# Low half stacked under the high half in the first inverse step: two products per group in place of three

## The chip, the cores and the metric
One core of a Trainium2 chip runs the whole program in one launch. The metric is device time in microseconds (us), the median of several executions. PE is TensorE (matmul), PEld its weight load, DVE VectorE, ACT ScalarE, POOL GpSimd, SP SyncE.

## The reference, cut to what matters
The program computes a Fourier attention layer on 128 images of 128 x 128, then an attention and an expert layer over tokens. The change touches only the inverse transforms of the first layer, which come three times (the projection, the first mixer layer and the second one):

```
def spectral_conv(x, w, out_shape):
    ...
    out_ft = out_ft.at[:, :, :mh, :mw].set(top)
    out_ft = out_ft.at[:, :, -mh:, :mw].set(bot)
    return jnp.fft.irfftn(out_ft, s=out_shape, axes=(-2, -1), norm='forward')
```

Of each image 34 x 34 real coefficients are kept (17 cosines and 17 sines in each direction). The inverse is two small matrix products: columns first (34 coefficients to 128 pixels), then rows.

## The kernel before, in words
`build` runs twelve stages, each a block with a barrier at its end. Three of them are `stage_inverse` with `kind` 'proj', 'mix1' and 'mix2'. Every value that needs more than half precision is held as two float16 parts, a high one and the low rest, and a product of two such values is three products: high by high, high by low, low by high.

A `stage_inverse` has this order:

- Head. In 'proj' alone DVE first sums the squares of the coefficients (L1345), PE spreads the sum over partitions, DVE and ACT make a scale of it. Then PE turns the coefficients, 34 transposes in nine banks (L1201). ACT copies each bank as float16 into `coefH` (L1251) and DVE writes the rest into `coefL` (L1355). Both lie on partitions 0 to 33 of the tile `spare`, one behind the other.
- First step, `first(q)`, for quads q = 0 to 10. A quad is four groups of three images (the last has fewer). Each group has three products with 34 contraction rows and 102 output rows: `coefH` by `colsH`, `coefH` by `colsL`, `coefL` by `colsH`, of 128 columns each, accumulated in one bank (L1166 to L1168). So a full quad has 12 matmuls, each with a weight load of its own.
- ACT copies a quad's bank as float16 to `halfH` (`half(q)`, L1223), and DVE writes the rest to `halfL` (L1284).
- Second step, `second(b)`: sets b = 3q to 3q + 2 of a quad, three products of 512 columns with 102 contraction rows (L1179 to L1181).
- DVE combines each set with the images (`combine(b)`, L1341) and takes statistics (L1308, or L1315). 'mix1' adds a Gelu on ACT (L1266), scaled copies on ACT (L1240), a forward transform on PE (L1189, 128 contraction rows, float32) and more copies. 'mix2' adds scaled copies on ACT (L1240) and sums on POOL.

The order on PE is written out by hand: `first(0)`, `first(1)`, then `second(b)` for all b, and after the last set of quad q comes `first(q + 2)`. In 'mix1' `forward(b - 2)` stands before it. ACT and DVE have `half(0)` and `half(1)` before all other work of the sets, and `half(q + 2)` after the last set of quad q. `first(q)` waits until DVE is done with the bank of quad q - 2 (`s.blow`).

The stationary operand of each of these products is the image data, and the table is what moves. `spare` is free at the start of each `stage_inverse`.

Of the kernel before, what the change touches and what calls it, by code (L numbers as in the profile page):

```python
# [31 lines left out]
P = 128  # L32
# [35 lines left out]
def tables():  # L68

    n = np.arange(P)[:, None]  # L70
    k = np.arange(K33)[None, :]
    dft = np.concatenate([np.cos(2 * np.pi * n * k / P), np.sin(2 * np.pi * n * k / P)], 1) / P
    dft[:, K33] = 0.0
    k = np.arange(K17)[:, None]
    idft = np.zeros((P, P))
    idft[:K17] = np.cos(2 * np.pi * k * n.T / P)
    idft[K17:FM] = np.sin(2 * np.pi * k * n.T / P)
    twice = np.where(np.arange(P) % K17 > 0, 2.0, 1.0)[:, None]
    batch = np.kron(np.eye(NB), np.ones((NT, NT))) / NT
    low = np.zeros((ROWS, K17))  # L80
    low[0:8, 1:9] = 2
    low[K17 + 1:K17 + 9, 1:9] = 2
    low[1:9, 0] = 2
    low[0, 0] = 1
    few = np.zeros((P, 5))
    for j, (re, im) in enumerate(((1, 0), (0, 1), (1, 0), (0, -1))):
        for i in range(9):
            few[9 * j + i, 0:2] = 64 * low[i, 0] * re, 64 * low[i, 0] * im
    few[36:39, 2:5] = 64 * np.eye(3)
    assert low.sum() == 2 * 136 + 1 and (low[0:8, 1:9] == 2).all() and (low[18:26, 1:9] == 2).all()  # L90
    var = np.zeros((2, K17, 2, K17))
    var[:, 1:, :, 1:] = 1
    var[0, 0, :, 1:] = 2
    var[:, 1:, 0, 0] = 0.5
    tie = np.arange(EXPERTS)[None, :] < np.arange(EXPERTS)[:, None]
    axis = np.full(P, P ** -0.5)
    axis[P - 1] -= 1.0
    house = np.eye(P) - 2.0 / (axis @ axis) * np.outer(axis, axis)
    house[:, P - 1] = 0.0
    pick = np.zeros((P, 2))  # L100
    pick[P - 1, 0] = 1.0

    def on_all(a):
        return np.broadcast_to(a.reshape(1, -1), (P, a.size))
    three = np.zeros((P, 3, P))
    for j in range(3):
        three[FM * j:FM * j + FM, j] = idft[:FM]
    parts = [('ident', np.eye(P)), ('tie', on_all(tie)), ('house', house), ('pick', pick), ('dft', dft), ('rows', idft), ('cols', idft * twice),
             ('batch', batch), ('low', few), ('var', on_all(var)),
             ('three', three.reshape(P, 3 * P))]  # L110
    at, where = 0, {}
    for name, a in parts:
        where[name] = (at, at + a.shape[1])
        at += a.shape[1]
    return np.concatenate([a for _, a in parts], 1).astype(np.float32), where
# [55 lines left out]
def memory(nc, ctx, where):  # L171
# [3 lines left out]
    def sb(scope, name, shape, dtype=F32):  # L175
        return scope.enter_context(nc.sbuf_tensor(name, shape, dtype))
# [19 lines left out]
    with ExitStack() as l0:  # L196
        m.a = sb(l0, "images_a", [P, NI, NW])
        c0 = where['dft'][0]
        m.tab = sb(l0, "table", [P, where['var'][1] - c0])

        def tab(name, rows=P):
            lo, hi = where[name]
            return m.tab[0:rows, lo - c0:hi - c0]
        m.dft = tab('dft')
        m.dft17 = m.dft.rearrange("p (s k) -> p s k", s=2)[:, :, 0:K17]
        m.rows, m.cols, m.batch, m.low, m.var = tab('rows', FM), tab('cols', FM), tab('batch'), tab('low'), tab('var')
        pair = sb(l0, "pair", [P, 2, 2 * NM])
        m.wraw = pair[0:64, 0, :].rearrange("p (r k c) -> p r k c", r=ROWS, c=2)
        m.weff = pair[0:64, 1, :].rearrange("p (c m) -> p c m", c=2)
        m.feat = pair[:, 0, :].rearrange("p (x y) -> p x y", x=FM)  # L210
        m.coef = pair[:, 1, :].rearrange("p (x y) -> p x y", x=FM)
        mixw = sb(l0, "mixer_weights", [P, 2 * NM])
        m.mixw = mixw[:, :].rearrange("p (r k c) -> p r k c", r=ROWS, c=2)
        m.feat0 = mixw[:, :].rearrange("p (x y) -> p x y", x=FM)
        f = sb(l0, "features", [P, FQ * FQ])
        m.ft = f[:, :].rearrange("p (x y) -> p x y", x=FQ)
        m.half17H, m.half17L = (f[:, P * K17 * i:P * K17 * (i + 1)].bitcast(F16).rearrange("p (t x) -> p t x", t=P)
                                for i in (0, 1))
        g = sb(l0, "spare", [P, HC * P])
        m.spare = g[:, :]  # L220
        m.gramT = g[:, :].rearrange("p (c t) -> p c t", c=HC)
        m.coefH, m.coefL = (g[0:FM, 2 * NI * FM // 4 * i:2 * NI * FM // 4 * (i + 1)].bitcast(F16)
                            .rearrange("p (t x) -> p t x", t=NI) for i in (0, 1))
        m.modes = sb(l0, "modes", [P, 2, NM])
        r = sb(l0, "transposed", [P, 1920])
        m.turned = r[:, :]
        m.modesT = r[:, 0:1280].rearrange("p (k c t) -> p k c t", k=5, c=2)
        m.wT = r[:, 1280:1920].rearrange("p (k c h) -> p k c h", k=5, c=2)
        m.stat = r[:, 0:768].rearrange("p (t s) -> p t s", t=P)
        m.aff = r[:, 768:768 + 8 * P].rearrange("p (k t) -> p k t", k=8)  # L230
        m.halfH = sb(l0, "half_inverse_high", [P, 2, GRP * NW], F16)[0:3 * FM]
        m.halfL = sb(l0, "half_inverse_low", [P, 2, GRP * NW], F16)[0:3 * FM]
        m.rowsH = sb(l0, "rows_high", [P, 3, P], F16)[0:3 * FM]
        m.rowsL = sb(l0, "rows_low", [P, 3, P], F16)[0:3 * FM]
        m.colsH = sb(l0, "cols_high", [P, P], F16)[0:FM]
        m.colsL = sb(l0, "cols_low", [P, P], F16)[0:FM]
        m.unity = sb(l0, "unity", [P, P])[:, :]
        norms = sb(l0, "norms", [P, 160])
        m.norms = [norms[:, 32 * i:32 * i + 32] for i in range(5)]
        m.rstd, m.back = m.norms[3], m.norms[4]  # L240
        dfts = sb(l0, "transform_pair", [P, 2, FQ], F16)
        m.dftH, m.dftL = dfts[:, 0, :], dfts[:, 1, :]
        m.dft17P = dfts[:, :, :].rearrange("p c (s k) -> p c s k", s=2)[:, :, :, 0:K17]
        m.ust = shared[:, :].rearrange("p (s t w) -> p s t w", s=2, t=GRP)
        m.tmp = m.modes[:, :, 0:GRP * NW]
# [105 lines left out]
def stage_tokens(nc, held, m, ins, const):  # L351
# [22 lines left out]
    with nc.Block() as block:  # L374
# [11 lines left out]
        def _(pool):  # L386
# [11 lines left out]
            pool.tensor_copy(m.colsH, m.cols).then_inc(s.split, 1)  # L398
            pool.wait_ge(s.split, 5)
            pool.tensor_tensor(m.rowsL, m.three, m.rowsH, ALU.subtract).then_inc(s.split, 1)  # L400
            pool.tensor_tensor(m.colsL, m.cols, m.colsH, ALU.subtract).then_inc(s.split, 1)
            pool.wait_ge(s.split, 7)

        @block.scalar
# [638 lines left out]
def stage_inverse(nc, held, m, kind, mix=None, ins=None):  # L1043


    s = semaphores(nc, held, "inverse_" + kind, "in0 in1 in2 in3 v sized rooted total scaled turned high low first bhigh "
                   "blow rows used lin ready saved forward copied halved weights cleared algebra affine added gstat partly")
    arrived = [s.in0, s.in1, s.in2, s.in3]
    sets = image_sets()
    up, down = m.col[:, 25:26], m.col[:, 26:27]  # L1050
# [62 lines left out]
    with nc.Block() as block:  # L1113
# [41 lines left out]
        def _(pe):  # L1155
            def first(q):
                if q == 0:
                    pe.wait_ge(s.high, len(COEF_BANKS))
                    pe.wait_ge(s.low, len(COEF_BANKS))
                if q >= 2:  # L1160
                    pe.wait_ge(s.blow, q - 1)
                for i, g in enumerate(range(4 * q, min(4 * q + 4, TRIPLES))):
                    n = min(3, NI - 3 * g)
                    part = m.ps[q % 2][0:n * FM, i * NW:i * NW + NW]
                    ch, cl = (c[:, 3 * g:3 * g + n, :].rearrange("p t x -> p (t x)") for c in (m.coefH, m.coefL))
                    pe.matmul(part, ch, m.colsH, start=True, stop=False)  # L1166
                    pe.matmul(part, ch, m.colsL, start=False, stop=False)
                    mm = pe.matmul(part, cl, m.colsH, start=False, stop=True)  # L1168
                mm.then_inc(s.first, 1)

            def second(b):
# [45 lines left out]
        def _(act):  # L1217
# [26 lines left out]
            if kind == 'proj':  # L1244
                act.wait_ge(s.scaled, 1)
                act.activation(down, m.col[:, 27:28], ACT.Sqrt).then_inc(s.rooted, 1)
                act.wait_ge(s.scaled, 2)
            for r, xs in enumerate(COEF_BANKS):
                act.wait_ge(s.turned, r + 1)
                n = len(xs)  # L1250
                act.activation(m.coefH[:, :, xs[0]:xs[0] + n], turned(r), ACT.Copy, scale=up[0:FM] if kind == 'proj' else 1.0).then_inc(s.high, 1)  # L1251
# [26 lines left out]
        def _(vec):  # L1278
# [47 lines left out]
            def combine(b):  # L1326
# [13 lines left out]
                    x = images(m.b, b)  # L1340
                vec.scalar_tensor_tensor(out=x, in0=y, scalar=gain, in1=x, op0=ALU.mult, op1=ALU.add).then_inc(s.used, 1)  # L1341

            if kind == 'proj':
                g = m.coef.rearrange("p x y -> p (x y)")
                vec.tensor_tensor_reduce(m.square, g, g, 1.0, 0.0, ALU.mult, ALU.add, m.col[:, 24:25]).then_inc(s.sized, 1)  # L1345
# [1308 lines left out]
```

## Time and profile before
| | us |
|---|---|
| median of 3 runs | 2337.13 (2336.1 to 2338.2) |
| the profiled execution | 2333.92 |
| its span, first instruction to last | 2331.8 |
| 'proj' | 228.6 to 293.5 of the span |
| 'mix1' | 310.5 to 444.5 |
| 'mix2' | 469.6 to 537.3 |
| all `first(q)`: 387 matmuls, busy | 98.9 |

How to read it: the program's time is some 2.1 us more than the span. Matmuls are pipelined, so the busy time of one is its latency, and the distance of two starts is what a matmul costs in a stream. The granted clock of TensorE in a stretch is given in parts of full speed: 0.5 is its lower level (1.2 GHz) and 1 its upper one (2.4 GHz).

### The profile page before, as it was taken

Reading aid. Unit: us, or ns where it says so; the run is one execution under the profiler, and the core shown is the slowest. Engines: PE = TensorE matmul, PEld = TensorE weight load, DVE = VectorE, ACT = ScalarE, POOL = GpSimd, SP = SyncE. Lnnn points to the kernel's source line nnn. Section 1 sums busy time; section 2 is a strip of 40 time slices with the busy share of each in tenths; the row PEclk is TensorE's granted clock in tenths of the full one; section 3 lists DMA queues with packets and bytes.
Section 4 is the critical chain, followed back from the end, with each engine's and each line's share of the span. In section 5 each row is a group of like instructions: output and inputs, shape, how many; then the busy total and the mean of one; then the engine's idle time right before and its main releaser. Section 6 shows DMA issues by size and latency. Waiting matters only on the chain. (4 is left out here: it accounts for less than half of the span.)

```text
span 2331.8 us, 30874 instructions
## 1 busy us (share of the span) xinstructions
PE 2060.5 (88%) x10374; PEld 1050.0 (45%) x10374; DVE 1884.1 (81%) x3617; ACT 1666.9 (71%) x2420; POOL 609.1 (26%) x754
## 2 busy tenths in 40 slices
PE   7776859685999999999999999999999999767778
PEld 7622346542444444444444444444444444333333
DVE  4667978886788888888889889889888888867776
ACT  1454146482888888888888888888888888676766
POOL 1035314355211201202202102102000001046669
PEclk9988755566999999999999999999999999888999
DMA  9004560000000000000000000000000000000101
GB/s 308 5 1 161 138 154 1 1 1 6 1 10 1 1 1 1 1 1 1 1 1 1 1 1 1 1 1 1 1 1 1 1 1 1 1 17 26 32 28 46
DMA packets 80833, 55.72 MB, mean 24 GB/s; under 512 B 11283, under 2 KB 78739, under 8 KB 79140
## 3 DMA queue, kind: packets, MB, share of 16 engines
q1 hardware_dynamic: 75476, 52.38, 7.5%
q10 hardware_dynamic: 5200, 1.38, 0.3%
q8 instruction: 82, 1.34, 0.2%
q14 instruction: 75, 0.61, 0.1%
HBM read 36.91 MB, written 16.78 MB: 23 GB/s over the span
## 5 line engine op out<-in xcount | busy, mean ns | idle before, releaser
L2026 ACT ACTIVATE inner<-banks,key_bias,scales 128x1024 f32<-128x1024 f32 x512 | 617.1, 1205 | 220.6 <-PE banks L1841 215.0
L2212 DVE TENSOR_TENSOR weights_low<-weights,weights_high 128x1024 f16<-128x1024 f32 x512 | 677.3, 1323 | 17.0
L2033 ACT ACTIVATE weights<-inner 128x1024 f32<-128x1024 f32 x512 | 541.0, 1057 | 18.5 <-DVE weights_low L2212 2.7
L2208 DVE CAST weights_high<-weights 128x1024 f16<-128x1024 f32 x512 | 371.8, 726 | 178.0 <-ACT weights L2033 164.2
L2321 POOL CAST sums_high<-sums 128x512 f16<-128x512 f32 x32 | 39.0, 1220 | 1081.3 <-ACT sums L2005 1063.3
L1841 PE MATMUL banks<-queries_high,keys_high 128*128 128x512 f16 x1024 | 305.5, 380 | 4.5 <-ACT inner L2026 4.5
L1841 PE MATMUL banks<-queries_low,keys_high 128*128 128x512 f16 x1024 | 305.5, 380 | 0.0
L1841 PE MATMUL banks<-queries_high,keys_low 128*128 128x512 f16 x1024 | 305.3, 380 | 0.0
L1856 PE MATMUL banks<-weights_high,tokens_low 128*128 128x512 f16 x1024 | 304.6, 379 | 0.0
L1856 PE MATMUL banks<-weights_high,tokens_high 128*128 128x512 f16 x1024 | 304.5, 379 | 0.0
L1856 PE MATMUL banks<-weights_low,tokens_high 128*128 128x512 f16 x1024 | 304.5, 379 | 0.0
L2519 ACT ACTIVATE scaled<-banks,gates 128x128 f32<-128x128 f32 x512 | 149.3, 395 | 88.3 <-PE banks L2481 88.2
L1841 PEld LDWEIGHTS banks<-queries_low,keys_high 128*128 128x128 f16 x1024 | 100.4, 98 | 121.5 <-issue 1.1
L1841 PEld LDWEIGHTS banks<-queries_high,keys_low 128*128 128x128 f16 x1024 | 100.4, 98 | 121.4 <-issue 1.1
L1856 PEld LDWEIGHTS banks<-weights_high,tokens_low 128*128 128x128 f16 x1024 | 100.2, 98 | 120.8
L1856 PEld LDWEIGHTS banks<-weights_high,tokens_high 128*128 128x128 f16 x1024 | 100.2, 98 | 120.8
L1856 PEld LDWEIGHTS banks<-weights_low,tokens_high 128*128 128x128 f16 x1024 | 100.2, 98 | 120.7
L2479 PE MATMUL banks<-expert_weights_high,normed_high 128*128 128x512 f16 x256 | 103.5, 404 | 56.9 <-DVE residual_and_scaled L2555 43.7
L1841 PEld LDWEIGHTS banks<-queries_high,keys_high 128*128 128x128 f16 x1024 | 97.1, 98 | 95.2 <-ACT inner L2026 5.1
L2584 POOL TENSOR_TENSOR scaled_halves<-scaled 128x256 f32<-128x256 f32 x128 | 94.2, 736 | 93.2 <-ACT scaled L2519 92.7
L2555 DVE SCALAR_TENSOR_TENSOR residual_and_scaled<-banks,gates,residual_and_scaled 128x128 f32<-128x128 f32 x384 | 110.0, 342 | 0.1
L2480 PE MATMUL banks<-expert_weights_low,normed_high 128*128 128x512 f16 x256 | 103.5, 404 | 0.0
(619 smaller groups left out, 3210.1 us busy)
## 6 DMA issues: line engine op xcount, KB each, us to landing
images_b<-in_x SPq DMA_DIRECT2D x32, 256.0 KB, 9.1
images_a<-in_x SPq DMA_DIRECT2D x8, 1024.0 KB, 9.8
mixed_scratch<-images_a SPq DMA_DIRECT2D x4, 2048.0 KB, 13.0
result<-group_result SPq DMA_DIRECT2D x32, 256.0 KB, 2.3
images_b<-mixed_scratch SPq DMA_DIRECT2D x10, 768.0 KB, 5.1
images_a<-in_x SPq DMA_DIRECT2D x10, 768.0 KB, 9.1
mixer_weights<-in_L_conv_mixer_w SPq DMA_DIRECT2D x4, 272.0 KB, 6.7
table<-tables ACTq DMA_DIRECT2D x1, 772.5 KB, 6.9
```

The lines of the kernel that those rows point to most:

```text
L1841: mm = pe.matmul(m.ps[2 * (t % 2) + h], key[:, par, part], query[:, q, 512 * h:512 * h + 512], start=(i == 0), stop=(i == 2))
L1856: mm = pe.matmul(m.ps[4 + h], value[:, par, k, :], weight[:, t % DEEP, 512 * h:512 * h + 512], start=(k == 0 and i == 0), stop=(k == KT - ...
L2026: act.activation(m.inner[:, t % 2, :], m.pair[t % 2], ACT.Exp, scale=m.fs[:, 1:2], bias=m.kb[:, c // QN % 2, k:k + 1]).then_inc(s.inner, 1)
L2033: act.activation(m.wt[:, t % 2, :], m.inner[:, t % 2, :], ACT.Exp).then_inc(s.outer, 1)
L2208: vec.tensor_copy(m.wH[:, t % DEEP, :], m.wt[:, t % 2, :]).then_inc(s.high, 1)
L2212: vec.tensor_tensor(m.wL[:, t % DEEP, :], m.wt[:, t % 2, :], m.wH[:, t % DEEP, :], ALU.subtract)\
L2321: after(pool.tensor_copy(m.oH[:, part], m.oS[:, part]))
L2479: pe.matmul(bank, m.lnH[:, t % RING, j, :], m.w8H[:, cols], start=True, stop=False)
L2480: pe.matmul(bank, m.lnH[:, t % RING, j, :], m.w8L[:, cols], start=False, stop=False)
L2519: o = act.activation(m.pb[:, n % 3, e, :], m.ps[ABANK[n % 2]][:, e * D:e * D + D], ACT.Copy, scale=m.gate[:, n, 4 + e:5 + e])
L2555: vec.scalar_tensor_tensor(out=m.u[:, n % 4, :], in0=m.ps[DBANK[n % 3]][:, e * D:e * D + D], scalar=m.gate[:, n, e:e + 1], in1=acc, op0=AL ...
L2584: pool.tensor_tensor(m.half[:, n % 2], m.pb[:, n % 3, 0:2], m.pb[:, n % 3, 2:4], ALU.add).then_inc(s.halved, 1)
```

## The change
`coefL` moves from partitions 0 to 33 to partitions 64 to 97, under `coefH` in the same columns of `coefW`. The column table holds its 34 rows twice, on partitions 0 and 64, and zeros between, so one product with 98 contraction rows gives high by high and low by high at once. Before ACT writes the first bank, DVE sets partitions 32 to 63 of `coefW` to zero in each of the three stages, 4352 float16 elements to a partition, and ACT waits for that (`s.blank`). The product `coefH` by `colsL` stays, with 34 contraction rows. A full quad has 8 matmuls in place of 12.

```
-    parts = [..., ('cols', idft * twice),
+    twofold = np.zeros((P, P))
+    twofold[:FM] = twofold[64:64 + FM] = (idft * twice)[:FM]
+    parts = [..., ('cols', twofold),
...
-        m.coefH, m.coefL = (g[0:FM, 2 * NI * FM // 4 * i:2 * NI * FM // 4 * (i + 1)].bitcast(F16)
-                            .rearrange("p (t x) -> p t x", t=NI) for i in (0, 1))
+        m.coefW = g[:, 0:NI * FM // 2].bitcast(F16).rearrange("p (t x) -> p t x", t=NI)
+        m.coefH, m.coefL = m.coefW[0:FM], m.coefW[64:64 + FM]
...
-                    ch, cl = (c[:, 3 * g:3 * g + n, :].rearrange("p t x -> p (t x)") for c in (m.coefH, m.coefL))
-                    pe.matmul(part, ch, m.colsH, start=True, stop=False)
-                    pe.matmul(part, ch, m.colsL, start=False, stop=False)
-                    mm = pe.matmul(part, cl, m.colsH, start=False, stop=True)
+                    ch, both = (c[:, 3 * g:3 * g + n, :].rearrange("p t x -> p (t x)") for c in (m.coefH, m.coefW[0:64 + FM]))
+                    pe.matmul(part, both, m.colsH, start=True, stop=False)
+                    mm = pe.matmul(part, ch, m.colsL, start=False, stop=True)
...
+            act.wait_ge(s.blank, 1)
             for r, xs in enumerate(COEF_BANKS):
                 act.wait_ge(s.turned, r + 1)
...
+            vec.memset(m.coefW[32:64], 0.0).then_inc(s.blank, 1)
             if kind == 'proj':
                 g = m.coef.rearrange("p x y -> p (x y)")
                 vec.tensor_tensor_reduce(m.square, g, g, 1.0, 0.0, ALU.mult, ALU.add, m.col[:, 24:25]).then_inc(s.sized, 1)
```

`colsH` grows to 98 partitions with it, and the float32 table and its copy too.

## Rows read from the trace of the kernel before

**Rows 1.** Windows view: us, busy of PE, PEld, DVE, ACT, POOL, granted clock.
```profile
228.60:293.50 64.90, 50.25 (x264) 24.92 (x264) 59.54 (x183) 13.41 (x23) 26.58 (x23) 0.71 0.52 139
310.50:444.50 134.00, 117.73 (x518) 86.46 (x518) 106.62 (x343) 86.86 (x216) 60.41 (x66) 0.51 0.28 68
469.60:537.30 67.70, 53.51 (x262) 25.17 (x262) 59.20 (x182) 59.45 (x149) 40.66 (x33) 0.68 0.00 1
```

**Rows 2.** Waits view, 'mix1' from 322 us: who for whom, us, times, longest.
```profile
ACT ow_stats_and_image_stage L1266 <- DVE modes L1341: 39.4, 31, 2.8
```

**Rows 3.** Timeline of DVE and PE in 'proj': start us, duration us.
```profile
276.51 0.74 DVE L1341 SCALAR_TENSOR_TENSOR images_b<-banks,small,images_b 128x512 f32<-128x512 f32 x1
281.40 0.74 DVE L1341 SCALAR_TENSOR_TENSOR images_b<-banks,small,images_b 128x512 f32<-128x512 f32 x1
...
279.07 0.63 PE L1181 MATMUL banks<-half_inverse_low,rows_high 102*128 102x512 f16 x1
```

**Rows 4.** Timeline of PE in 'proj', quad 3, clock at its upper level.
```profile
247.40 0.38 PE L1181 MATMUL banks<-half_inverse_low,rows_high 102*128 102x512 f16 x1
247.71 0.26 PE L1166 MATMUL banks<-cols_high,spare 34*102 34x128 f16 x1
...
248.36 0.22 PE L1168 MATMUL banks<-cols_high,spare 34*102 34x128 f16 x1
248.51 0.39 PE L1179 MATMUL banks<-half_inverse_high,rows_high 102*128 102x512 f16 x1
```

**Rows 5.** Timeline of PE in 'mix1', clock at its lower level.
```profile
328.80 0.31 PE L1167 MATMUL banks<-cols_low,spare 34*102 34x128 f16 x1
328.91 0.31 PE L1168 MATMUL banks<-cols_high,spare 34*102 34x128 f16 x1
329.15 0.61 PE L1179 MATMUL banks<-half_inverse_high,rows_high 102*128 102x512 f16 x1
...
329.98 0.63 PE L1181 MATMUL banks<-half_inverse_low,rows_high 102*128 102x512 f16 x1
330.40 1.76 PE L1189 MATMUL banks<-table,ow_stats_and_image_stage 128*128 128x34 f32 x8
331.97 0.62 PE L1179 MATMUL banks<-half_inverse_high,rows_high 102*128 102x512 f16 x1
...
340.30 1.76 PE L1189 MATMUL banks<-table,ow_stats_and_image_stage 128*128 128x34 f32 x8
341.99 0.34 PE L1166 MATMUL banks<-cols_high,spare 34*102 34x128 f16 x1
```

**Rows 6.** Timeline of the head of 'proj': PE, ACT, DVE.
```profile
238.88 0.23 PE L1166 MATMUL banks<-cols_high,spare 34*102 34x128 f16 x1 [2.49 <-DVE spare L1355]
...
239.76 1.26 ACT L1223 CAST half_inverse_high<-banks 102x512 f16<-102x512 f32 x2 [2.07 <-PE banks L1168]
...
242.44 0.75 DVE L1341 SCALAR_TENSOR_TENSOR images_b<-banks,small,images_b 128x512 f32<-128x512 f32 x1 [0.70 <-PE banks L1181]
```

**Rows 7.** Timeline of the head of 'mix1': PE and ACT.
```profile
319.05 0.23 PE L1166 MATMUL banks<-cols_high,spare 34*102 34x128 f16 x1 [1.78 <-DVE spare L1355]
...
312.42 0.60 ACT L1251 ACTIVATE spare<-banks 34x512 f16<-34x512 f32 x1 [0.25 <-PE banks L1201]
...
321.11 0.59 ACT L1223 CAST half_inverse_high<-banks 102x512 f16<-102x512 f32 x1 [0.60 <-PE banks L1168]
```

**Rows 8.** Timeline of the head of 'mix2': PE and ACT.
```profile
477.48 0.23 PE L1166 MATMUL banks<-cols_high,spare 34*102 34x128 f16 x1 [2.10 <-DVE spare L1355]
...
478.36 1.26 ACT L1223 CAST half_inverse_high<-banks 102x512 f16<-102x512 f32 x2 [2.14 <-PE banks L1168]
```

**Rows 9.** Timeline of DVE: memsets of other stages.
```profile
98.48 0.17 DVE L651 MEMSET images_b<- 128x132 f32 x1
...
552.39 0.06 DVE L1722 MEMSET value_map_low<- 128x1 uint32 x1
```

**Rows 10.** Windows view, start of the last stage, columns as in the first group.
```profile
2016.00:2100.00 84.00, 47.87 (x295) 24.64 (x294) 57.40 (x203) 51.27 (x152) 31.73 (x58) 0.80 0.04 13
```

## What the change will do to the time: the prediction on record
> **What bounds the kernel now.** I read the windows view first, one window for each `stage_inverse` [rows 1]. In 'proj' DVE is busy for 59.5 of 64.9 us and TensorE's mean granted clock is 0.71. In 'mix2' DVE (59.2) and ACT (59.5 of 67.7) lead; the rest of ACT's window is the head. In 'mix1' PE looks busiest (117.7 of 134 us), but that is latency at a clock of 0.51. The waits view corrects it: what ACT waits for in its Gelu is DVE's combine, 31 times, 39.4 us [rows 2], so 'mix1' turns in a ring of ACT and DVE. I read it so: PE works ahead of the other two in all three stages once the sets run. In 'proj' the timeline of DVE gives the period of a quad, 4.89 us, from combine to combine (276.51 to 281.40) without idle, and the product for the combine at 281.40 had ended at 279.70, 1.70 us early [rows 3]. So matmuls saved inside a stage shorten nothing; what is on the path of each stage is its head, where ACT and DVE can only wait for `first(0)` and `first(1)`.
>
> **What the removed products are worth.** 129 of 387 matmuls go. In a stream two of them start 0.055 us apart at the upper clock (247.71 to 248.36, eleven steps; the first takes 0.10, the others 0.055) [rows 4] and 0.11 (0.106 in the mean of a block) at the lower one [rows 5]. All 129 would be some 7 to 14 us of PE if nothing else changed.
>
> **What the added rows do.** The timeline of PE shows a cost where the number of contraction rows changes. From a 34-row product to the 102-row one behind it: 0.15 in place of 0.055 at the upper clock [rows 4], 0.24 in place of 0.106 at the lower one [rows 5]. From 102 rows to 34: 0.31 [rows 4], where a product of 512 columns is followed after 0.21 (half of the 0.42 at the lower clock from 329.98 to 330.40 [rows 5]). So a change costs some 0.093 us at the upper clock and 0.135 at the lower one. Is it the rows, or the kind of load, or the wait on a semaphore? [rows 5] hold the controls. 102 to 128 rows, float16 to float32 (329.98 to 330.40) costs nothing extra; 128 to 102 behind eight L1189 takes 1.57 (330.40 to 331.97), and the same eight before a 34-row product 1.69 (340.30 to 341.99), 0.12 more. So it is the 34 rows against the more than 100.
>
> The new group runs 98 rows, 34 rows, 98, 34. I take 98 as 102, its nearest row in the trace, so every one of the 8 products of a quad but the first comes behind a change, and so does the 102-row product behind them. A step then is 0.055 + 0.093 = 0.148 us at the upper clock, 0.106 + 0.135 = 0.24 at the lower. A quad in the middle of a stage:
> - upper clock: before 0.31 + 11 x 0.055 + 0.15 = 1.07, after 0.21 + 8 x 0.148 = 1.39: 0.33 more
> - lower clock: before 0.56 + 11 x 0.106 + 0.24 = 1.97, after 0.43 + 8 x 0.24 = 2.35: 0.40 more
>
> Two products cost more than three. The Trainium skill has rules for both sides. TensorEngine Tiling (Array Packing), Key Properties, says that changing the tiling mode drains the engine, and has a mode with 64 rows for contractions up to 64; by that 34 and 98 rows are two modes, which is what speaks against this change. That rule gives no time; the rows above do, and they agree with it.
>
> **The middle of the stages: 0.** What hides 0.33 to 0.40 us a quad is the lead of PE. In 'proj' the smallest lead is that 1.70 us [rows 3], behind four quads that ran at the lower clock; with 4 x 0.40 off it is 0.1 left. 'mix2' has over 2 us before each `half(q)` and over 1.9 before each combine in the same views. In 'mix1' the first product behind `first(q)` has 2.0 us before its combine, and PE then idles for DVE before the next quad. If the cover goes it costs up to 0.40 a quad.
>
> **The heads.** Let T be the start of `first(0)`. At the upper clock a product ends 0.22 us behind its start and ACT starts on it some 0.03 to 0.05 later.
> - 'proj': ACT's `half(0)` starts at T + 0.88 (238.88 to 239.76) [rows 6], that is 11 steps and 0.27. After it is 7 x 0.148 + 0.27 = 1.31: +0.43. The first combine waits for PE's second step (idle 0.70 [rows 6]), which waits for `half(0)` on both engines, so this goes through. `first(1)` ends at T + 2.44, still ahead of the second step at T + 2.67. +0.4.
> - 'mix1': ACT's `half(1)` starts at T + 2.06 (319.05 to 321.11), 0.60 late for `first(1)` [rows 7]; the clock fell within the block. DVE must have `half(1)` before the first linear pass and combine, so here 24 products became 16: 15 steps, 5 of them at the upper clock, 0.74 + 10 x 0.24 and 0.34 to ACT's start = 3.5: +1.45.
> - 'mix2': `half(0)` and `half(1)` are back to back now, the second at T + 1.55 (478.36 + 0.63 + 0.04 - 477.48) [rows 8]; after, 15 x 0.148 + 0.26 = 2.48: +0.93. Behind it ACT has its scaled copies without a gap to the end of the stage, so all of it goes through. At the lower clock it would be 15 x 0.24 + 0.34 = 3.94 against 2.78, +1.2.
>
> Sum of the heads: 0.43 + 1.45 + 0.93 = 2.8 us.
>
> **The memset.** The trace has no memset of this size. Nearest rows: 132 float32 elements in 0.17 us on DVE, 1 element in 0.06, so 0.83 ns an element; and a zero of two float16 went out as one uint32 element [rows 9]. I take 4352 float16 as 2176 words: 0.06 + 2175 x 0.83 ns = 1.87 us. The upper bound is 4352 elements, 3.7 us; the lower one 0.95, since no row excludes two words in a step. I take the middle, which is what the uint32 row stands nearest to. The Trainium skill, VectorE: DVE Perf Modes, Zero memsets can be issued as uint32, says that a memset takes a cycle for an element whatever its type, and gives the form with words; at the 0.96 GHz it names that would be 2.3 us as an estimate, 0.4 more than by the rows.
> - 'proj': the memset is DVE's first instruction, and behind it are the sum of squares, PE's spreading, the scale, ACT's first bank and, since PE waits in order, the transposes too. All on the path: +1.9.
> - 'mix1': DVE would be idle, but ACT waits for `blank`. ACT takes a bank in 0.60 and then waits 0.25 for PE [rows 7], so banks come 0.85 us apart, the first at 311.57. It moves to about 312.4; ACT and DVE can take banks 0.6 apart or less, so by the fourth the 0.8 is caught up: 0.
> - 'mix2': the same delay of 0.8, but the clock rises earlier and the banks come faster, so DVE enters its unbroken run 0.1 late: +0.1.
>
> POOL and the DMA queues get nothing new; the wider copy of the column table has the same elements per partition: 0.
>
> **Sum.** 2.8 + 1.9 + 0.1 = 4.8 us. Against the profiled execution: span 2331.8 to 2336.6, time 2333.9 to 2338.7. That execution was 3.2 us below the median of the runs, and I give the change to the median: 2337.1 + 4.8 = 2341.9.
>
> **Rivals.**
> - *The alternation is free* (98 and 34 rows follow each other like 34 and 34). Then the heads lose 4 x 0.055 in 'proj' and 'mix2' and 0.87 in 'mix1', 1.3 together, against 2.0 of memset: 2337.8. For it: no row has 98 rows, or a change within one accumulation. Against: both directions cost the same in [rows 4] and [rows 5] with three kinds of neighbours. The Trainium skill, TensorE: Matmul & The Clock Gate, Small-K row of its table of advice, says a product with 32 rows takes as long as one with 128; by that alone the result would be this one. Chance 0.17.
> - *The memset runs by half words*: 3.7 us in 'proj', and 'mix1' and 'mix2' no longer catch up (DVE's nine banks of 0.6 from 314.8 end 1.1 and 1.9 late): 6.7 in place of 2.0, 2346.6. Against it is the uint32 row [rows 9]. Chance 0.07.
> - *The cover in 'proj' goes.* At the lower clock a quad of PE is 5.40 us now and 5.80 after, against DVE's 4.89. Four such quads leave 0.1; six or seven, should the clock stay low longer, put DVE behind by 1 to 3 us: about 2344.9. Chance 0.10.
> - *Faster: the clock of the last stage.* In its first 84 us the granted clock is 0.80 [rows 10]. Everything up to it moves by 5 us, and where the clock falls could move. It must give back 4.8 us to be faster at all and 9.5 to be so measurably. Were those 84 us bound by PE and the clock at 0.92, they would take 73: 11 less, 2331. Against: three runs lie within 2.1 us. Chance 0.04.
> - My forecast: 0.62, itself 2340.5 to 2343.5.
>
> **The numbers.** 0.2% is 4.7 us, about what a measurement of this kernel can tell from no change, so slower begins at 2341.8, in the middle of my forecast. Slower: 0.36 of its 0.62, and 0.07 and 0.10, 0.53. Same: the other 0.26 and 0.17 of the free alternation, 0.43. Faster 0.04. The range takes in the free alternation below and the half-word memset only in part above: 2337.5 to 2346.
>
> **What would show it.** Starts inside `first(q)` 0.15 apart at the upper clock and 0.24 at the lower show the price of the change of rows; 0.055 and 0.106 refute it. One memset of 1.9 us ahead of L1345's successor, as uint32, shows the second term. `half(1)` at T + 2.5 to 3.5 in 'mix1' and 'mix2' shows the heads, and combines 4.89 us apart in 'proj' that the middle stays covered. I would be wrong most by the memset's price in 'proj', or by a clock that stands otherwise at a head.

## The result and the profile after

The changed kernel takes 2348.84 us (median of 6 runs, 2347.71 to 2355.96) against 2339.22 us (6 runs, 2336.1 to 2340.83) of the kernel before in the same comparison. The ratio is 1.0047, with a 95% interval of 1.0034 to 1.0061: slower by about 11 us, with 9.6 between the two medians. A second measurement of the same kernel gave 2350.22 and 1.0052 (1.0036 to 1.0068). The direction was foreseen, the size was not: +4.8 was forecast, and the result lies above the range. (The forecast of 2341.9 stood on a median of 2337.1 from three runs of the kernel before; with six it is 2339.2, so 2.1 of the 6.9 us between forecast and result are not the change's.)

The windows view of the changed kernel, the three `stage_inverse` one after the other, columns as in [rows 1]:
```profile
231.00:304.70 73.70, 59.50 (x221) 28.03 (x221) 64.14 (x187) 13.32 (x23) 27.01 (x23) 0.66 0.46 122
320.50:456.80 136.30, 124.75 (x475) 85.94 (x476) 107.99 (x344) 86.41 (x217) 60.48 (x66) 0.51 0.28 67
481.90:552.20 70.30, 55.58 (x219) 25.52 (x219) 60.83 (x183) 59.06 (x149) 40.71 (x33) 0.74 0.00 1
```
Each stage can be cut at four events that every kernel here has: its start, PE's first transpose, the first product of `first(0)`, DVE's first combine and DVE's last. The pieces in us, from the timelines of PE, ACT and DVE of the two profiled executions:

| | before | after | more | forecast |
|---|---|---|---|---|
| 'proj': start to first transpose | 1.96 | 5.66 | 3.70 | 1.87 |
| 'proj': transposes / head / middle | 8.25 / 3.56 / 50.47 | 8.26 / 4.82 / 53.12 | 0.0 / 1.26 / 2.65 | 0 / 0.43 / 0 |
| 'mix1': the same three | 8.53 / 5.34 / 115.31 | 8.36 / 7.60 / 115.31 | -0.2 / 2.26 / 0 | 0 / 1.45 / 0 |
| 'mix2': the same three | 7.79 / 5.14 / 53.19 | 8.36 / 6.85 / 53.18 | 0.6 / 1.71 / 0 | 0.1 / 0.93 / 0 |

The head is the piece from the first product to the first combine, the middle the piece from the first combine to the last. Together they are 259.5 us before and 271.5 after: 12.0 of the 15.0 us between the two spans (2331.8 and 2346.8). 2.4 more lie ahead of 'proj', which starts at 231.11 in place of 228.67; the last experiments come back to them.

The entry of 'proj', DVE and POOL:
```profile
231.62 1.87 DVE L1345 MEMSET spare<- 32x2176 uint32 x1 [2.29 <-PEq L891]
233.52 2.73 DVE L1348 CUSTOM_DVE_ANT_0 images_a<-pair 128x1156 f32<-128x1156 f32 x1
```
```profile
231.11 1.06 POOL L1081 MEMSET mixer_weights<- 128x1156 f32 x1 [8.80 <-POOLq L891]
232.13 3.15 POOL L1082 TENSOR_SCALAR features<-pair 128x1156 f32<-128x1156 f32 x1
```
The memset is one instruction of 2176 words and 1.87 us, as forecast to the hundredth. But it cost more than itself. It starts 0.51 us behind POOL's first instruction, where DVE's sum of squares stood 0.08 behind it before (228.75 and 228.67). And the sum of squares, 1.36 us before, takes 2.73, because it now lies beside POOL's arithmetic, first L1082 and from 235.37 on L1083.

The head of 'proj', PE:
```profile
245.02 0.23 PE L1168 MATMUL banks<-cols_high,spare 98*102 98x128 f16 x1 [2.60 <-DVE spare L1358]
245.18 0.26 PE L1169 MATMUL banks<-cols_low,spare 34*102 34x128 f16 x1
245.37 0.26 PE L1168 MATMUL banks<-cols_high,spare 98*102 98x128 f16 x1
...
247.24 0.34 PE L1168 MATMUL banks<-cols_high,spare 98*102 98x128 f16 x1
247.52 0.34 PE L1169 MATMUL banks<-cols_low,spare 34*102 34x128 f16 x1
247.79 0.35 PE L1168 MATMUL banks<-cols_high,spare 98*102 98x128 f16 x1
```
Products start 0.185 to 0.19 apart at the upper clock and 0.27 to 0.28 at the lower. [rows 4] and [rows 5] had 0.055 and 0.106, the forecast 0.148 and 0.24. Sixteen products now take 3.32 us (245.02 to 248.34). What DVE has at this head:
```profile
249.06 0.69 DVE L1286 TENSOR_TENSOR half_inverse_low<-banks,half_inverse_high 102x512 f16<-102x512 f32 x1 [1.16 <-ACT half_inverse_high L1224]
249.84 0.75 DVE L1343 SCALAR_TENSOR_TENSOR images_b<-banks,small,images_b 128x512 f32<-128x512 f32 x1
255.05 0.69 DVE L1286 TENSOR_TENSOR half_inverse_low<-banks,half_inverse_high 102x512 f16<-102x512 f32 x1 [0.97 <-ACT half_inverse_high L1224]
261.03 0.69 DVE L1286 TENSOR_TENSOR half_inverse_low<-banks,half_inverse_high 102x512 f16<-102x512 f32 x1 [0.82 <-ACT half_inverse_high L1224]
```
The first combine starts at 249.84. DVE's part of `half(1)` ends at 249.75, and the product that the combine needs at 249.80 (started at 249.17, 0.63 long): two routes that end together, and both begin at the last of the sixteen products. The forecast had the route over `half(0)`, whose DVE part was done at 247.91, before PE began its second step at 248.34. And DVE is idle ahead of `half(q)` in two further quads, which begin 5.98 us apart (255.05 to 261.03) where [rows 3] showed 4.89 without idle.

### The profile page after: what moved, and what is told of

It is laid out like the page before. It is cut to its first block and busy times, and to the rows that moved or that the text cites. A ratio compares the mean times of both kernels' runs of the same rounds, so it can differ in the third digit from the quotient of the medians.

```text
span 2346.8 us, 30621 instructions
## 1 busy us (share of the span) xinstructions
PE 2080.4 (89%) x10245; PEld 1054.4 (45%) x10245; DVE 1888.7 (80%) x3620; ACT 1666.1 (71%) x2420; POOL 609.5 (26%) x754
## 6 DMA issues: line engine op xcount, KB each, us to landing
table<-tables ACTq DMA_DIRECT2D x1, 772.5 KB, 5.8
```

## The experiments

**What do unequal rows cost, and does anything else of the change?** Two kernels on the changed one. The first runs both products of a group over 98 rows; rows 34 to 97 of the second table are zero, so the result is the same sum. The second keeps 98 and 34 rows but turns the order round in every other group, so that there are half as many changes of rows.

`full98`:
```diff
-        m.colsL = sb(l0, "cols_low", [P, P], F16)[0:FM]
+        m.colsL = sb(l0, "cols_low", [P, P], F16)[0:64 + FM]
-            pool.tensor_tensor(m.colsL, m.cols[0:FM], m.colsH[0:FM], ALU.subtract).then_inc(s.split, 1)
+            pool.tensor_tensor(m.colsL, m.cols, m.colsH, ALU.subtract).then_inc(s.split, 1)
...
+            pool.memset(m.colsL[64:64 + FM], 0.0).then_inc(s.split, 1)
-                    mm = pe.matmul(part, ch, m.colsL, start=False, stop=True)
+                    mm = pe.matmul(part, both, m.colsL, start=False, stop=True)
```


> The changed kernel, with both products of a group over 98 contraction rows: the low column table is padded with zeros on rows 34 to 97, so the sums are the same, there are still 8 products in a quad and no change of rows at all. Theory A (changes of the number of rows cost PE time; in the trace of the changed kernel 0.13 us each at the upper clock and 0.17 at the lower): steps inside a quad are 0.055 and 0.106 us again, the heads become shorter than those of the kernel before, the middle of 'proj' stays covered, and what is left against the kernel before is the memset and what it brings in 'proj' (3.7 us) less some 1.3: ratio to before 1.001, 2.4 us slower. Rival B (the alternation is not what costs; memset and clock are): steps unchanged from the changed kernel, 10 us slower than before, ratio 1.004 to 1.005.

Measured: 2340.84 us against 2338.16, ratio 1.0015 (1.0002 to 1.0027). Its products in a quad of 'proj' at the upper clock, and in one at the lower:
```profile
248.84 0.22 PE L1170 MATMUL banks<-cols_high,spare 98*102 98x128 f16 x1
248.90 0.22 PE L1171 MATMUL banks<-cols_low,spare 98*102 98x128 f16 x1
...
254.77 0.31 PE L1170 MATMUL banks<-cols_high,spare 98*102 98x128 f16 x1
254.88 0.31 PE L1171 MATMUL banks<-cols_low,spare 98*102 98x128 f16 x1
```
0.06 and 0.11: the steps of the kernel before, with nearly three times the rows. The heads are 3.53, 4.89 and 4.72 us, not one longer than before, and the middle of 'proj' is 50.47 again. Of the 12.0 us 3.1 are left: the entry of 'proj' costs 3.70, and the heads give a little back.

`mirror`:
```diff
-                    pe.matmul(part, both, m.colsH, start=True, stop=False)
-                    mm = pe.matmul(part, ch, m.colsL, start=False, stop=True)
+                    if i % 2 == 0:
+                        pe.matmul(part, both, m.colsH, start=True, stop=False)
+                        mm = pe.matmul(part, ch, m.colsL, start=False, stop=True)
+                    else:
+                        pe.matmul(part, ch, m.colsL, start=True, stop=False)
+                        mm = pe.matmul(part, both, m.colsH, start=False, stop=True)
```


> The changed kernel, but every second group gives its 34-row product first, so the rows go 98, 34, 34, 98, 98, 34, 34, 98 and a quad has 4 changes in place of 8. Same 8 products, same memset. Theory A: a quad's PE time falls by 4 x 0.13 (upper clock) or 4 x 0.17 (lower clock), the result lies about half way between the changed kernel (+10 us against before) and the one with 98 rows throughout (+2.4): +6 us, ratio 1.0025. If it is not the changes of rows but the weight load of 98 rows or the 98-row product itself, steps stay as in the changed kernel and so does the time.

Measured: 2346.95 us, ratio 1.0032 (1.0019 to 1.0044), between the two. Its timeline of PE shows both sorts of step beside each other:
```profile
247.92 0.22 PE L1172 MATMUL banks<-cols_low,spare 34*102 34x128 f16 x1
248.07 0.26 PE L1173 MATMUL banks<-cols_high,spare 98*102 98x128 f16 x1
248.16 0.22 PE L1169 MATMUL banks<-cols_high,spare 98*102 98x128 f16 x1
248.31 0.26 PE L1170 MATMUL banks<-cols_low,spare 34*102 34x128 f16 x1
```
A change costs a step of 0.15, and the step of equal rows behind it 0.09 to 0.10 in place of 0.055. At the lower clock they are 0.24 and 0.135 to 0.14, where the equal step was 0.106. So a change is paid twice. Where every step is a change both seem to fall on one step, for the sum comes out: 0.055 + 0.093 + 0.04 = 0.188, the 0.187 of the changed kernel. Eight of them are 1.5 us a quad, the mixture of `mirror` 4 x 0.145 + 4 x 0.095 = 0.96, the equal rows of `full98` 0.44.

**What does the memset cost alone?** The kernel before with nothing but the memset and ACT's wait for it.

`memset_only`, on the kernel before:
```diff
+            act.wait_ge(s.blank, 1)
             for r, xs in enumerate(COEF_BANKS):
...
+            vec.memset(m.blank, 0.0).then_inc(s.blank, 1)
             if kind == 'proj':
```


> The kernel before, its three products and its layout, with the memset on DVE at the start of each stage and ACT waiting for it (partitions 32 to 63 of the same columns; the computation is whole). Theory A: in 'proj' 1.87 us of memset, and DVE's sum of squares, which now runs beside POOL's first arithmetic, takes 2.7 us in place of 1.36, so +3.2 to 3.7 us there; 'mix1' 0, 'mix2' 0.1 to 0.6; in all +3.8 us, ratio 1.0016. If the sum of squares is slow for another reason (the new layout), it stays at 1.36 and the whole is +2.0.

Measured: 2345.07 us, ratio 1.0028 (1.0013 to 1.0043), +6.4 in the stages. That is more than was expected, but only 3.7 of it is at the memset:
```profile
234.81 1.87 DVE L1345 MEMSET spare<- 32x2176 uint32 x1 [1.88 <-PEq L890]
236.71 2.73 DVE L1348 CUSTOM_DVE_ANT_0 images_a<-pair 128x1156 f32<-128x1156 f32 x1
```
The other 2.7 are the middle of 'proj' (52.16) and the head of 'mix2' (6.23). The middle of 'proj' is not the memset's: the unchanged kernel has 52.17 too when its clock is low there (below). Nor is the 1.1 in the head of 'mix2' a wait for the memset. There the steps of PE go from 0.056 to 0.106 at the fourth product, and `half(1)` comes at T + 2.65 in place of T + 1.55; `full98`, with the same memset and the clock up through that head, has 4.72. Whether the memset had a part in where the clock fell is not shown.

**Do the heads alone carry it?** `full98`, with the 34-row product back in `first(0)` and `first(1)` of each stage.

`alt_heads`, on `full98`:
```diff
-                    mm = pe.matmul(part, both, m.colsL, start=False, stop=True)
+                    mm = (pe.matmul(part, ch, m.colsL[0:FM], start=False, stop=True) if q < 2 else
+                          pe.matmul(part, both, m.colsL, start=False, stop=True))
```


> As the kernel with 98 rows throughout, but in the first two quads of each stage the second product of a group keeps its 34 rows: only the heads alternate. It parts the cost of the heads from that of the middle. Theory A: heads 15 changes each, with the time of the first combine in 'proj' 1.3 to 1.5 us, in 'mix1' 2.3 and in 'mix2' 1.7 us later than in the kernel before, and the middle of 'proj' not bound by PE: against the kernel with 98 rows throughout +5 to 7 us, and 2 to 3 us faster than the changed kernel. If the middle of the stages is where the loss is, it equals the kernel with 98 rows throughout within 2 us.

Measured: 2348.96 us, ratio 1.0041 (1.0027 to 1.0055). In its profile the heads are 4.83, 6.39 and 6.67 us, 4.8 more than in `full98` (1.3, 1.5 and 1.95), and the middles are those of before, 50.47, 115.33 and 53.19. 16 of a stage's 86 products thus carry 4.8 of the 8.9 us that lie between `full98` and the changed kernel in the stages. Of the rest the middle of 'proj' has 2.65 and the head of 'mix1' 1.2. The times do not part the two: 2 to 3 us faster than the changed kernel was expected, and `alt_heads` is as slow as that (1.0041 and 1.0047), though its profiled run (2345.65) is one of its faster ones. So by the runs the heads may carry all of the difference to `full98` (1.0015); the share of the middle stands on single profiles.

**Two kinds of rows, or a cost for each row?** The second product over 64 rows, or over 66, the added ones zero in `cols_low`, which grows with them. Both have a change in the number of rows at every step.

`rows64` and `rows66` (there `[0:66]`):
```diff
-                    mm = pe.matmul(part, ch, m.colsL, start=False, stop=True)
+                    more = m.coefW[0:64, 3 * g:3 * g + n, :].rearrange("p t x -> p (t x)")
+                    mm = pe.matmul(part, more, m.colsL, start=False, stop=True)
```


> The changed kernel, but the second product of a group has 64 contraction rows (30 rows of zeros in its column table; the sums are the same), so rows go 98, 64, 98, 64. If the cost hangs on the difference 34 to 98 it should shrink; if 64 rows belong to the same kind as 34, the steps stay at 0.15 to 0.19 us at the upper clock and 0.24 to 0.27 at the lower. A kernel with 66 rows is to follow, which should be free of it.

> As the kernel with 64 rows in the second product, but with 66: rows go 98, 66, 98, 66. If the engine has two kinds of product, up to 64 rows and above, the steps inside a quad are 0.055 us at the upper clock and 0.106 at the lower, as with 98 rows throughout; if every change of the number of rows costs, they stay at 0.15 to 0.19 and 0.24 to 0.27.

Measured, a single run each: 2347.68 us and 2343.83 us. Since single runs of the kernel before lie between 2332.45 and 2344.91, the verdict rests on the steps and the stages. `rows64`:
```profile
246.39 0.26 PE L1168 MATMUL banks<-cols_high,spare 98*102 98x128 f16 x1
246.57 0.26 PE L1170 MATMUL banks<-cols_low,spare 64*102 64x128 f16 x1
246.76 0.26 PE L1168 MATMUL banks<-cols_high,spare 98*102 98x128 f16 x1
```
`rows66`:
```profile
248.10 0.22 PE L1170 MATMUL banks<-cols_high,spare 98*102 98x128 f16 x1
248.16 0.22 PE L1172 MATMUL banks<-cols_low,spare 66*102 66x128 f16 x1
248.22 0.22 PE L1170 MATMUL banks<-cols_high,spare 98*102 98x128 f16 x1
```
0.185 against 0.06, and in the stages +9.2 against +2.7. Two rows more take the whole cost away. There are two kinds of products, and the border lies between 64 and 66 rows. The Trainium skill, TensorEngine Tiling (Array Packing), Key Properties, says that a change of tiling mode drains the engine, and its Tiling Modes have one of 64 rows. The two runs agree with it, if a plain product of up to 64 rows counts as that mode, which is my reading and not the page's.

**Can POOL take the memset?** Three kernels move it from DVE to POOL, ahead of POOL's own first work in each stage; the first two also ask whether the gain adds to that of equal rows.

`after_pool` on the changed kernel, `full98_pool` on `full98`:
```diff
+            pool.memset(m.coefW[32:64], 0.0).then_inc(s.blank, 1)
+            pool.wait_ge(s.blank, 1)
...
-            vec.memset(m.coefW[32:64], 0.0).then_inc(s.blank, 1)
```


> The changed kernel with its memset on POOL, the 34-row products as they are. Theory A: the alternation alone: the 3.7 us of the start of 'proj' go and the heads and the middle keep their cost, so 7 us slower than before, ratio 1.003. If the memset were most of the loss: 1.001 or less.

> 98 rows throughout, and the memset of the three stages on POOL, as its first instruction, in place of DVE. Theory A, refined (98 rows throughout cost nothing on PE; the memset costs 3.7 us at the start of 'proj', of which half is the memset and the rest what it pushes DVE's sum of squares into): the transposes of 'proj' start 2.0 to 2.2 us behind the barrier again as in the kernel before (5.74 with the memset on DVE), the sum of squares takes 1.4 us, the heads are as short as with 98 rows throughout: 3.7 us less than that, 0.5 to 1 us faster than the kernel before, ratio 0.9997. If the loss of 98 rows throughout came from elsewhere, the ratio stays at 1.0015.

Measured: `after_pool` 2351.70 us, ratio 1.0041 (1.0027 to 1.0055); `full98_pool` 2343.89, ratio 1.0013 (1.0000 to 1.0026). The entry of 'proj' is 1.96 again in both, but 'mix1' and 'mix2' gave most of it back: from first transpose to first product 9.69 us in place of 8.36. So neither expectation came true (1.003 and 0.9997). The cause is in `full98_pool`, in the timelines of POOL and ACT at the start of 'mix1':
```profile
317.77 3.72 POOL L1142 MEMSET spare<- 32x4352 f16 x1 [50.08 <-POOLq L2630]
```
```profile
321.52 4.26 ACT L1257 ACTIVATE spare<-banks 34x512 f16<-34x512 f32 x9 [6.86 <-POOL spare L1142]
```
On POOL the same memset goes out as 4352 float16 elements and takes 3.72 us, and ACT's first bank waits for it. It starts 3.75 us into the stage, where it started 2.38 in with the memset on DVE.

`words_pool`, on `full98_pool`, the same bytes written as float32:
```diff
-            pool.memset(m.coefW[32:64], 0.0).then_inc(s.blank, 1)
+            pool.memset(m.spare[32:64, 0:NI * FM // 2], 0.0).then_inc(s.blank, 1)
```


> 98 rows throughout, and the memset on POOL as 2176 float32 zeros in place of 4352 float16 ones. POOL's memsets of the kernel before cost 0.83 ns an element, so 1.87 us in place of the 3.72 that the float16 one took on POOL. Theory A: 'proj' as with the float16 memset on POOL (66.2 us) less up to 0.3, 'mix1' and 'mix2' as with 98 rows throughout (133.5 and 68.0): the three stages together 267.5 us against 267.9 in the kernel before, so no measurable difference from the kernel before, ratio 0.9995 to 1.0005. If it is 1.0013 again, part of the loss has nothing to do with the memset's place or the rows.

Measured: 2336.19 us against 2339.95, ratio 0.9988 (0.9977 to 0.9999). It is the one version faster than the kernel before, by about 3 us where no difference was expected; the interval nearly touches 1, so the gain is small and not sure. POOL and DVE at the entry:
```profile
231.68 1.90 POOL L1142 MEMSET spare<- 32x2176 f32 x1 [8.79 <-POOLq L893]
231.76 1.36 DVE L1351 CUSTOM_DVE_ANT_0 images_a<-pair 128x1156 f32<-128x1156 f32 x1 [1.86 <-PEq L893]
```
1.90 us, and the sum of squares is back at 1.36. In the stages it has 1.5 us less than before, at the heads (3.10, 4.53, 4.97). That is what 129 saved products are worth where the rest is off the path, by one profile; against the heads of the kernel before profiled again (3.75, 4.82, 5.14, below) it is 1.1.

**Is it POOL's arithmetic that doubles the sum of squares?** The changed kernel, with POOL in 'proj' held until the sum of squares is done.

`pool_waits`:
```diff
             if kind == 'proj':
+                pool.wait_ge(s.sized, 1)
```


> The changed kernel with one wait more: POOL starts its arithmetic in 'proj' only when DVE's sum of squares is done. If POOL working at the same time is what doubles that sum, it takes 1.36 us again and the transposes start 4.4 us behind the barrier in place of 5.74. If it stays at 2.73, the cause lies in the memset ahead of it or in the layout.

Measured, a single run: 2356.22 us. POOL is late with its own work there, and the three stages are as long as in the changed kernel all the same (+12.0): the middle of 'proj' has 53.08 and its head 5.87. The entry:
```profile
238.53 1.87 DVE L1346 MEMSET spare<- 32x2176 uint32 x1 [1.66 <-PEq L891]
240.43 1.36 DVE L1349 CUSTOM_DVE_ANT_0 images_a<-pair 128x1156 f32<-128x1156 f32 x1
241.86 1.06 POOL L1081 MEMSET mixer_weights<- 128x1156 f32 x1 [12.01 <-DVE small L1349]
```
1.36 again behind the same memset, and the entry falls from 5.66 to 4.29. So 1.37 of the 3.70 is the overlap with POOL. The slowing goes both ways: POOL's L1083, which ended beside the sum of squares in the changed kernel, took 3.37 us there, and the same operation 2.65 in the kernel before. The Trainium skill, GPSIMD Engine Reference, Specifications, says that POOL shares its interfaces to SBUF with VectorE, with contention for instructions with two inputs in SBUF; the sum of squares has `pair` as both of its inputs, and the row agrees. The last 0.46 (4.29 - 1.96 - 1.87) is the later start of DVE's first instruction: it stays when POOL is idle, and its cause is open.

**How far does the same kernel move?** The changed kernel timed again, and the kernel before profiled again, neither edited.

> The changed kernel once more, for the spread of its time on the same chip as the other two and a second profile. Its three stages should take 277 to 280 us (279.9 in its first profile), of which the middle of 'proj' is 50.6 to 53.1 by where the clock falls; ratio 1.0045.

> The kernel before once more, for a second profile of it. If the middle of 'proj' depends on where the clock falls in the kernel before too, it may differ from 50.47 us (up to 52.2, as with the memset alone); the stages of scores and mixing, which no kernel here changes, should take 22.9 + 90.0 or 25.4 + 92.0 us.

Measured: 2350.22 us and 2340.91 us (a single run). In the stages `after_again` has +13.0 where the first profile had +12.0, with 54.23 for the middle of 'proj', above what was expected. `before_again` has +0.3, with 52.17 in place of 50.47 for the middle of 'proj' and 4.82 in place of 5.34 for the head of 'mix1'. 4.7 us lie ahead of 'proj', which starts at 233.38 in place of 228.67, all of them behind 111 us. A window of both in which the clock differs, first the kernel before as first profiled, then again:
```profile
118.00:150.00 32.00, 19.22 (x69) 7.33 (x70) 19.98 (x34) 12.02 (x34) 4.47 (x4) 0.73 0.00 0
```
```profile
118.00:150.00 32.00, 18.78 (x61) 6.38 (x62) 18.34 (x31) 9.83 (x29) 1.95 (x2) 0.57 0.00 0
```
One program, granted 0.73 and 0.57 of the clock over the same 32 us, and PE gets 61 of 69 instructions done. A part of the 2.65 us in the middle of 'proj' is likewise within what two executions of one kernel differ by.

The 2.4 us ahead of 'proj' are something else. They are there at 56 us already, in the first stage, where the clock is at 1.00 in both kernels and DVE waits for images. DVE of the kernel before and of the changed one:
```profile
53.61 6.29 DVE L521 BATCH_NORM_STATS2 modes<-images_a 128x6 f32<-128x128 f32 x32 [4.77 <-DMA images_a<-in_x]
```
```profile
55.82 6.29 DVE L523 BATCH_NORM_STATS2 modes<-images_a 128x6 f32<-128x128 f32 x32 [5.78 <-DMA images_a<-in_x]
```
At that place `before_again` is 0.1 us early and `memset_only` 0.6 late, while the eleven profiles of kernels with the column table of 98 rows are 0 to 4.0 us late, nine of them by 1.2 or more. So a part of the 2.4 may belong to the change, though its transfers of the table are as large (772.5 KB) and its copies as long as before. Whether it does, and by what route, is open.

## Why the direction was right and the size was not

**The alternation: right in kind, half the size.** The step that failed is "So a change costs some 0.093 us at the upper clock and 0.135 at the lower one." It prices only the step across the change. The step behind it is long too, and I had it in hand: "the first takes 0.10, the others 0.055" [rows 4]. I took that as a start of the stream and left out its 0.045. `mirror` shows both parts. A change costs about 0.135 us at the upper clock and 0.17 at the lower, so the steps are 0.187 and 0.274 in place of 0.148 and 0.24. The rest of that paragraph held: the three controls in [rows 5] pointed at the rows, and `rows64` and `rows66` settle it: not every difference in rows, but the border at 64. The free alternation, given 0.17, is refuted.

**The heads: 5.2 in place of 2.8.** With the measured steps the arithmetic of 'mix2' comes near: from the first product to the fifteenth 2.59 (490.42 to 493.01), one step of 0.28 at the lower clock and 0.38 to ACT's start bring `half(1)` to T + 3.25 against the forecast 2.48. In 'mix1' the clock had fallen by the third product, not the sixth, and `half(1)` stands at T + 4.33 against 3.5. In 'proj' also the route was wrong: "The first combine waits for PE's second step" still held, but that step no longer waits for `half(0)`. It waits for the end of the sixteen products (T + 3.32, forecast T + 2.44), and so does `half(1)`, which ends with it: +1.26 in place of 0.43. A part of it all is where the clock stood, which in 'mix1' was low from the third product on. `alt_heads`, with the upper clock through nearly all of the heads of 'mix1' and 'mix2', has `half(1)` at T + 3.12 and T + 3.08, 1.5 to 1.6 behind the T + 1.55 of the kernel before at that clock.

**The memset: its price right, its place wrong.** 1.87 us in words was exact, the 2.3 beside it 0.4 too much, and the half-word rival (0.07) fell on DVE, though it came true on POOL. The failed step is "All on the path: +1.9". It took the work behind the memset as unchanged in length, but it moved under POOL's arithmetic and doubled: +1.37, shown by `pool_waits`, and 0.46 for a later start. I had read the queues of POOL and found that they "get nothing new", and did not ask what DVE would now lie beside. Nor was the delay of `blank` caught up. With the memset on DVE it is 8.36 or 8.37 us from first transpose to first product in 'mix1' and in 'mix2' in every profile. The kernel before has 8.53 and 7.79 in its first profile and 7.80 and 7.54 in its second, so "by the fourth the 0.8 is caught up: 0" holds against the first alone, and in 'mix2' it was 0.57 or 0.82 in place of 0.1.

**The middles: right in 'mix1' and 'mix2', not in 'proj'.** 115.3 and 53.2 us in every kernel. In 'proj' a quad at the lower clock became longer by 0.59, not 0.40 (by the forecast's own sum 0.38, 2.35 - 1.97):
```profile
257.71 0.63 PE L1182 MATMUL banks<-half_inverse_low,rows_high 102*128 102x512 f16 x1
258.14 0.31 PE L1168 MATMUL banks<-cols_high,spare 98*102 98x128 f16 x1
258.38 0.34 PE L1169 MATMUL banks<-cols_low,spare 34*102 34x128 f16 x1
...
260.31 0.61 PE L1180 MATMUL banks<-half_inverse_high,rows_high 102*128 102x512 f16 x1
```
2.60 us from L1182 to L1180, where the forecast had 2.35 and the kernel before has 2.01. A quad of PE is then 5.98 us, not 5.80. But the step that failed is "What hides 0.33 to 0.40 us a quad is the lead of PE": it took the smallest lead of one profile, in which the first quads ran at the upper clock, for one that is always there. Right behind the head PE has none. In the changed kernel the first three quads of combines are 5.98, 5.99 and 5.20 us apart and all others 4.89 or less, though three more quads (from 279.84 on) run at the lower clock. In `rows64` and `after_pool`, with the same steps, the clock is low in three quads of the middle alone, and these middles are 50.61 and 50.68. The kernel before pays the same way when the clock is low at once:
```profile
247.25 0.75 DVE L1341 SCALAR_TENSOR_TENSOR images_b<-banks,small,images_b 128x512 f32<-128x512 f32 x1 [0.89 <-PE banks L1181]
...
252.66 0.75 DVE L1341 SCALAR_TENSOR_TENSOR images_b<-banks,small,images_b 128x512 f32<-128x512 f32 x1
```
These are the first two quads in `before_again`, 5.41 us apart (247.25 to 252.66); three such quads make its 52.17. So the rival "The cover in 'proj' goes" (0.10) came true in its time, 2.65 us inside its 1 to 3, and by luck, for it asked for six or seven quads at the lower clock one behind the other. How much the change costs here depends on where the clock falls: `after_again`, low in the first three quads, has 54.23. Over these profiles the middle of 'proj' is between 0 and 3.8 us more than 50.47, and single profiles can't give its mean.

**The sum.** With 3.7 for the entry, 5.2 for the heads, 2.65 for the middle and 0.4 for the banks it is 12.0 in the stages of the first pair of profiles, against 9.6 between the medians. The two need not agree: the kernel before moves by 1.7 in its middle of 'proj' alone. Of the 12.0, equal rows take away 8.9 (`full98`), and the memset on POOL in words another 4.5 (`words_pool`). The rival of a faster last stage (0.04) showed nothing: DVE's last combine of 'mix2' stands 14.6 us later (550.44 against 535.81) and the span is 15.0 longer, so over the 1,800 us behind it 0.4 was added and none given back. (In the fourteen profiles that part is 1795.3 to 1798.2 us long, with 2.2 between the two of the kernel before.)

## What to carry to other kernels

Count products by their rows before stacking a contraction: at this size each change of kind (from up to 64 rows to 66 and more, or back) costs 0.13 us at the upper clock and 0.17 at the lower, where a further product costs 0.055 and 0.106. So fill up with zero rows until all are of one kind, which here cost next to nothing. Price a change by the step behind it as well as by the step across it. An instruction put at the head of a stage is paid in full and also shifts what follows under other engines' work: look at whose rows that work comes to lie beside, and give a memset to an idle engine, in 32-bit words. And read the lead of an engine at the start of a stage, and from more than one profile, before counting on it.

## What the runs showed of the hardware

- The kind of product, by its rows, is what costs: 98 and 64 rows in turn start 0.185 us apart, 98 and 66 in turn 0.06, 98 and 98 0.055 to 0.06, at the upper clock.
- A change also lengthens the equal step behind it, 0.055 to 0.095 us and 0.106 to 0.137.
- A zero memset of float16 goes out as words on DVE (2176 elements, 1.87 us) and not on POOL (4352 elements, 3.72 us; as float32 1.90).
- DVE's sum of squares over 1156 elements takes 1.36 us beside a memset of POOL and 2.73 beside its tensor_scalar and tensor_tensor.
- The same program had its clock at 0.73 in one execution and 0.57 in another over 118 to 150 us, and stood 4.7 us later at the start of 'proj'. That this is most of what lies between its lowest and highest run (2332.45 and 2344.91) is argued, not shown.
- 'proj' pays for a low clock in its first quads and not in later ones: combines are 5.4 us apart there before and 5.98 after, 4.89 in the rest.
- Open: why DVE's first instruction of 'proj' starts some 0.5 us later when it is the memset, and why images reach DVE up to 4.0 us later in the first stage of the kernels with the larger table.
